# Products with V for three key tiles at a time instead of two, and the work around them regrouped: a four-layer cross-attention kernel on one core

## The reference

```python
q = hidden_states @ Wq            # 2048 x 1024
k = encoder_hidden_states @ Wk    # 1601 x 1024
v = encoder_hidden_states @ Wv
logits = einsum('bhqd,bhkd->bhqk', q, k) * scale + col_bias
probs = softmax(logits, axis=-1)
out = einsum('bhqk,bhkd->bhqd', probs, v)
out = out @ Wo + bo
return out + residual
```

## Time and profile before

| | before |
|---|---|
| median of 3 runs | 4974.72 us (4973.66 to 4977.84) |
| the profiled execution | 4978.01 us, span 4976.2 us |
| TensorE / VectorE / ScalarE / GpSimd busy | 94% / 66% / 46% / 53% of the span |
| TensorE clock granted, mean | 0.96 |

### The profile page before, as it was taken

One profiled execution on the slowest core, in us unless ns is written; L12 is line 12 of the kernel. 1 busy time (PEld: TensorE's weight loads), 2 busy tenths in 40 slices (PEclk: granted clock), 3 DMA queues, 4 the chain that ended last, 5 costly groups with the idle time before them and its releaser, 6 DMA issues.

```text
span 4976.2 us, 56529 instructions
## 1 busy us (share of the span) xinstructions
PE 4669.4 (94%) x20473; PEld 2878.2 (58%) x20473; DVE 3276.1 (66%) x5099; ACT 2305.6 (46%) x4066; POOL 2621.8 (53%) x1266
## 2 busy tenths in 40 slices
PE   8999789999999798898897899999998899999999
PEld 7888555556555354444445555565554565555554
DVE  3321377777777676776654777777776777777777
ACT  3222444445544345555463444455544454444443
POOL 0000367778887200100103677788874587777775
PEclk9999899999999879999998999999999899999999
DMA  4465812222220101000106122222205221122210
GB/s 162 156 208 166 253 24 54 55 55 55 55 54 18 34 16 24 17 17 17 24 8 222 24 54 55 55 55 55 55 17 162 85 54 48 39 55 55 55 40 18
DMA packets 101063, 332.33 MB, mean 67 GB/s; under 512 B 15333, under 2 KB 33765, under 8 KB 88810
## 3 DMA queue, kind: packets, MB, share of 16 engines
q1 hardware_dynamic: 100784, 328.72, 24.4%
HBM read 193.15 MB, written 120.31 MB: 63 GB/s over the span
## 4 chain that ended last, share of the span: by engine, by line
PE 87%; DMA 4%; DVE 4%; issue 2%; SPq 1%; ACT 1%; POOL 0%; DVEq 0%; ACTq 0%
PE ST L806 13%; PE SS L790 12%; PE ST L807 11%; PE OA L817 11%; PE OB L817 10%; PE OA L947 4%; PE SS L907 4%; PE SS L838 3%; PE ST L926 3%; DMA q_parts<-stl 2%; DMA QX<-QS 2%; PE SS L827 2%; PE OB L907 2%; DVE xacc L1335 1%; PE SS L926 1%
## 5 line engine op out<-in xcount | busy, mean ns | idle before, releaser
L694 POOL TENSOR_TENSOR acc<-acc,P 128x1024 f32<-128x1024 f32 x900 | 2153.6, 2424 | 696.4 <-DVE acc L1321 651.3
L1101 ACT ACTIVATE P<-ST 128x512 f32<-128x512 f32 (+1 forms) x2496 | 1468.3, 598 | 1373.6 <-PE ST L807 1218.7
L1297 DVE TENSOR_REDUCE mpart<-SS 128x1 f32<-128x400 f32 (+1 forms) x3072 | 1631.8, 570 | 657.8 <-PE SS L790 580.7
L790 PE MATMUL SS<-KS,QS 68*128 68x400 f32 (+1 forms) x3072 | 1037.6, 373 | 52.4 <-DVE mpart L1297 43.2
L806 PE MATMUL ST<-QX,KX 128*128 128x512 f32 (+1 forms) x2496 | 1041.1, 417 | 8.3 <-DMA QS<-mrow 8.3
L807 PE MATMUL ST<-QS,KS 69*128 69x512 f32 (+1 forms) x2496 | 997.1, 399 | 0.0
L790 PEld LDWEIGHTS SS<-KS,QS 68*128 68x128 f32 x3072 | 588.9, 192 | 256.2 <-DVE mpart L1297 66.4
L806 PEld LDWEIGHTS ST<-QX,KX 128*128 128x128 f32 (+1 forms) x2496 | 468.3, 188 | 391.7 <-issue 290.9
L817 PE MATMUL OA<-P,Vp 128*64 128x512 f32 (+1 forms) x2496 | 661.0, 608 | 0.0
L817 PE MATMUL OB<-P,Vp 128*64 128x512 f32 (+1 forms) x2496 | 642.9, 593 | 0.0
L703 POOL TENSOR_TENSOR On<-Oraw,R 32x512 f32<-32x512 f32 x64 | 81.1, 1268 | 849.3 <-DVE R L1406 701.6
(11 more groups left out here) (220 smaller groups left out, 4617.1 us busy)
## 6 DMA issues: line engine op xcount, KB each, us to landing
QX<-q_parts SPq DMA_DIRECT2D x96, 512.0 KB, 11.5
KX<-k_parts SPq DMA_DIRECT2D x48, 801.0 KB, 9.5
q_parts<-sth SPq DMA_DIRECT2D x96, 256.0 KB, 4.2
q_parts<-stl SPq DMA_DIRECT2D x96, 256.0 KB, 4.2
QS<-q_parts SPq DMA_DIRECT2D x48, 512.0 KB
v_tiles<-sv SPq DMA_DIRECT2D x24, 832.0 KB, 6.5
Vp<-v_tiles SPq DMA_DIRECT2D x24, 832.0 KB, 7.7
k_parts<-skh SPq DMA_DIRECT2D x48, 400.5 KB, 4.8
```

Source lines behind the costliest of these rows:

```text
L694: gp.tensor_tensor(out, out, P[0:k, slot(H, t), q, :], ALU.add).then_inc(pool_a, 1)
L790: pe.matmul(SS[at % 3][:, 0:w], QS[H % 3][0:SROWS, qt * 128:(qt + 1) * 128], KS[H % 3][0:SROWS, o:o + w], start=True, stop=True).then_inc( ...
L1101: act.activation(P[0:k, slot(H, t), j, :], ST[n % 3][0:k, :], ACT.Exp, scale=SCALE).then_inc(act_p, 1)
L1297: dve.tensor_reduce(mpart[H % 2][:, i // len(KCH), c:c + 1], SS[RING_AT["s", H, i] % 3][:, 0:w], AX.X, ALU.max).then_inc(dve_ss, 1)
```

## The change

Groups of V products hold three key tiles, so a head has 5 steps (3, 3, 3, 3 and 1 tiles). What hangs on the step number moves with it: the sums stand behind the first step, the reciprocals at the ends of steps 1 and 2 instead of 2 and 3. VectorE's two additions leave the ends of steps 0 and 1 (`dve_tiles(h)[g:g + 1]`) and stand behind units 3 and 9 of step 0, which has 12 units. The bias pass is gone; in the first pair of a layer the output addition is a `scalar_tensor_tensor` with the bias as its scalar.

```diff
-PV = [range(t, min(t + 2, KT)) for t in range(0, KT, 2)]
+PV = [range(t, min(t + 3, KT)) for t in range(0, KT, 3)]
...
-    if h % 2 == 1 and h >= 3 and g < 2 and u % 2 == 0:
+    if h % 2 == 1 and h >= 3 and g < 2 and u % 2 == 0 and u < 8:
...
 def takes_sums(h, g):
-    return g == 1 and h > 0
+    return g == 0 and h > 0
...
             def add_output(n, i):
                 dve.wait_ge(pe_o, 8 * n + i + 1)
-                x = xacc[:, i % CT, i // CT * 512:i // CT * 512 + 512]
-                dve.tensor_tensor(x, SS[RING_AT["o", n, i] % 3][:, :], x, ALU.add).then_inc(dve_ss, 1)
-
-            def add_bias(l, i):
-                x = xacc[:, i % CT, i // CT * 1024:i // CT * 1024 + 1024]
-                dve.tensor_scalar(x, x, bo[:, l, i % CT:i % CT + 1], None, ALU.add).then_inc(dve_bo, 1)
+                x, bank = xacc[:, i % CT, i // CT * 512:i // CT * 512 + 512], SS[RING_AT["o", n, i] % 3]
+                if n % PAIRS == 0:
+                    dve.wait_ge(d_small, 16 * (BIG + 1))
+                    dve.scalar_tensor_tensor(x, bank[:, :], bo[:, n // PAIRS, i % CT:i % CT + 1], x, ALU.add, ALU.add)\
+                        .then_inc(dve_ss, 1)
+                else:
+                    dve.tensor_tensor(x, bank[:, :], x, ALU.add).then_inc(dve_ss, 1)
...
                         for i in tiles:
                             s_max(H + ahead, i)
+                        if h + 1 < HEADS and g == 0 and u in (3, 9):
+                            add(H, 1 + u // 9)
                     if g == ROW_STEP - 1 and h + 1 < HEADS:
                         head_max(H + 1)
-                    if h + 1 < HEADS:
-                        for t in dve_tiles(h)[g:g + 1]:
-                            add(H, t)
-                    else:
+                    if h + 1 == HEADS:
                         for t in PV[g]:
                             if t in dve_tiles(h):
                                 add(H, t)
-                    if h == 0 and 2 <= g < 4:
-                        for i in range(2):
-                            add_bias(l, 2 * (g - 2) + i)
-                    if h > 0 and 2 <= g < 4:
-                        reciprocals(H - 1, g - 2)
+                    if h > 0 and 1 <= g < 3:
+                        reciprocals(H - 1, g - 1)
```

More of the change, by code:

```diff
@@ L340, in attention_layers @@
         act_o, dve_r, pool_on = sem("act_o"), sem("dve_r"), sem("pool_on")
-        dve_bo = sem("dve_bo")
         pe_out, dve_out, d_out = sem("pe_out"), sem("dve_out"), sem("d_out")
```

## The result

The changed kernel takes 5088.5 us (5085.7 to 5104.4, 4 runs) beside 4976.0 us for the kernel before (4973.7 to 4977.8, 4 runs): 1.0233 times as long, 95% interval 1.0211 to 1.0255. It is slower, as forecast, but by 113 us instead of 28, and outside the range. The profiled execution took 5104.35 us with a span of 5102.6; it is the longest of the four, 16 us above their median, so differences taken from its trace are somewhat larger than those of the medians.

The account below looks back on a forecast made before the run. TensorE, busy 94% of the span, was taken as the bound. Terms -28.6 - 46 + 77 + 20 + 6 = +28.4 us on the profiled 4978.0 gave 5006, or 5003 against the median; range 4945 to 5045.

Parts of the forecast that it names:

- Term 1: Groups of V products, 42 middle heads: seven groups become five, 0.34 us saved a group, -28.6 us.
- Term 2: First head of each layer without the bias pass: 64.8 us against 80.2, -46 us, bounds -36 to -54.
- term 3: Step 0 of middle heads: first addition delays tile 9, stalling TensorE 1.8 or 1.9 us, +77 us, bounds +50 to +118.
- Term 4: Last head of a layer: sums come 6.7 us later, +20 us for three layers, +6 for lost clock.
- 5, GpSimd: GpSimd ends 1.4 us before the next head's first addition, so nobody waits: 0.
- B: Unit 6 of step 0: the ring swallows the addition, term 3 is 0, 4926 us; decides at 1.2 us a head; chance 0.20.
- C: First addition meets unfinished GpSimd: 4.05 instead of 2.35 us, 1.7 us more a head, 5040 us; chance 0.12.
- D: Terms cancel: stall 1.2 us, or first head gains more and last loses less; 4975 within 10 us; chance 0.10.

Follow-up runs that it names:

- busy in its wait: Changed kernel plus six redundant score products in each of 42 middle heads, ahead of the unit before the stalled maximum tile: 5009.5 us, ratio 1.0076.
- the run with the fold alone: Kernel before with only the bias folded into the first pair's output additions and no bias pass: 4917.3 us, ratio 0.9883.
- the kernel where it was provoked: Kernel before, two-tile groups, with only the first addition moved from the end of step 0 to behind unit 3: 5271.7 us, ratio 1.0599.

## Why the forecast was wrong

| term | forecast | measured | from |
|---|---|---|---|
| 1, tiling changes, middle heads | -28.6 | -28.8 | both additions at the end of step 0, against before |
| 2, first heads | -46 | -35.3 | after, against before |
| 3, stall in the middle heads | +77 | +71.7 | busy in its wait, against both additions at the end |
| 3, clock behind that stall | not counted | +96.6 | after, against busy in its wait |
| 4, last heads and behind | +26 | +24.5 | after, against before |
| 5, GpSimd | 0 | 0 | no first addition over 1.22 us |

With -2.3 us ahead of the first head these are the 126.4 us between the spans. By the medians, the run that is busy in its wait recovers 79 us, of the 85 by which the forecast missed.

**The step that failed** is the sum of term 3, "24 x 1.8 + 18 x 1.9 = +77 us". The walk to it was right: tile 9, in unit 6, behind a reduction that stands behind the addition; 1.6 us in short heads and 1.7 in long ones, against 1.8 and 1.9. But I priced the stall as lost time alone and left TensorE's clock at 1.00 afterwards. I had read 0.51 behind the stall of the first head and used it in terms 2 and 4, and did not ask it of the 42 waits that I was adding; the prediction gives no reason for that. The clock fell behind most of them, and a short head lost 3.1 us more, twice the stall. (The Trainium skill, TensorE: Matmul & The Clock Gate, "A second HAM failure mode: psum-queue depth-cycling", tells of a kernel that cycles through PSUM banks, whose TensorE idles briefly between groups of products and whose clock swings between the two levels for it; the trace agrees, with 1.47 us idle and then 0.56, though not every such wait here had it, and I had not weighed it.) The runs with redundant products show that the loss hangs on the wait: with the wait filled it is gone in all 42 heads, with the wait filled in part as well, and with the same work elsewhere it stays in 25. Neither the upper bound of the term (+118) nor the range took it in; with the clock the sum would have been 28 + 97 = 125 us, 5103 beside the 5104.35 of the profiled execution (the errors of the other terms cancel).

**Term 1** came out within a us, from four small differences of one group, and its mechanism with it: the same four losses stand in the rows around a three-tile group. The run that shows it also holds the moved additions; that these cost nothing there is seen from 90.00 busy us of 90.00.

**Term 2** is two errors. The bias pass was worth 60 us, as the run with the fold alone shows (19.7 to 20.7 us a layer); the prediction's "some 9 us" for it, an estimate from the SBUF page's rule, has no working there and came out far too low. The additions inside step 0 then gave back 27 us of it (first heads from 177.0 to 204.1). I had 64.8 us a head, 5.4 above the 59.4 without stalls. The waits are only 3.0; that gaps which I added up overlap with slack in the ring is my reading, not shown. A further 13.7 us at the lower clock (20.5 in that head, where the kernel with both additions at the end of step 0 has 6.8) stand beside the other 5.4. I had named that as a bound ("-12 if the long steps bring the clock down"), and it is the case: -11.8 a layer.

**Term 4**: the sums stand 6.8 us later (72.5 against 65.7), 6.7 forecast, and 1.4 us a layer are left for the clock and the rest, where I took 2. That VectorE idles with additions queued behind the output additions is borne out: with the key-tile additions drawn forward, the same work is done 5.6 us earlier.

**The rivals.** B is false where the change puts the first addition (1.6 us, above its deciding 1.2) and true for the second one. C is false here, and cost 5.7 us of wait in a short head and 3.7 in a long one in the kernel where it was provoked. Its price of 1.7 us a head was read too low: the 4.05 us of the earlier trace rows are 2.9 for the first half, which met GpSimd, and 1.2 for the second, which did not; where both meet it they take 6.6. D fell with the clock.

**Still open** is what beside the wait decides. Six of the 42 heads kept the clock with the same wait, and 17 with the same wait and more products elsewhere. The low stretch was 3.4 us in long heads and 6.8 or 10.2 in short ones. A single wait of 2.07 us idle, right ahead of the V products in the first heads, left the clock at 1.00 three times, while waits of 0.3 to 0.55 us in a row were enough in 9 short heads. So the length of one wait does not decide alone; no run here varied what stands before and behind the wait by itself.

## What to carry to other kernels

Where TensorE is the bound and its clock is full, price a new wait twice: once as the wait, once as what the clock may lose behind it. Take the second from a row of the same trace that shows the clock behind any wait, and carry it as a bound, since not every wait here brought the clock down. Put work of another engine that TensorE's ring will wait for behind the last reduction of a step, under products that need nothing from it; if a wait can't be avoided, filler work in it (5005 and 5010 us) or several short waits (5029) cost less here than one long one (5088). An instruction that is dear beside its size is first to be moved, not removed: here the bias pass cost nothing measurable two steps earlier (4916.0 us, and 4917.3 without it).

## What the runs showed of the hardware

- TensorE, busy for the rest of the head, was granted 1.2 GHz for 3.4 to 10.2 us within 2.1 us of the end of one wait of 1.6 to 1.9 us, in 36 of 42 heads of the profiled execution, and with six more products elsewhere in 25. With 0.9 to 1.2 us (three products in the wait) it was in none, and with waits of 0.2 to 0.7 us in a row in 9. Behind a wait of 2.2 us ahead of V products (first heads, first addition behind unit 9) it kept 2.4 GHz, three times of three.
- VectorE additions with two SBUF inputs took 1.22 us a half beside an idle GpSimd, 3.1 to 3.4 us a half where they met its additions (6.63 for two). A bias addition took 0.74 us beside an idle GpSimd, and 18.1 us where it met a row of its additions: it ended 0.6 us after the last of them.
- SCALAR_TENSOR_TENSOR with a bank of PSUM, a scalar and SBUF took 0.75 us, and TENSOR_TENSOR without the scalar 0.69.
